# Attention over 8 batches: the expert correction applied to every tile's rows, or from the third batch on to the picked rows in DRAM

## What is computed

```
x = x + 0.5 * ffn(layernorm(x))
x = x + attn(layernorm(x))
x = x + 0.5 * ffn(layernorm(x))
```

```
merged = einsum('bked,bke->bed', tok, vals)
h = gelu([merged, 1] @ w1)
o = [h, 1] @ w2
out = zeros_like(x).at[b, flat_idx].add(o * vals)
```

## Time and profile before

| | |
|---|---|
| Median of 3 runs | 2297.79 us (2296.61 to 2299.26) |
| The profiled execution, its own time | 2299.73 us |
| Its span, first to last instruction | 2298.0 us |
| Gate | to about 170 us |
| Experts, first pass | about 170 to 930 us |
| Attention | about 930 to 1660 us |
| Experts, second pass, and the end | about 1660 to 2298 us |

### The profile page before, as it was taken

How to read it: one execution, slowest core, us unless ns; L and a number is a source line. 1 busy time by engine, 2 the same in 40 slices (tenths; PEclk the granted TensorE clock), 3 DMA queues, 4 the chain that set the end, 5 groups by cost and what they waited for, 6 DMA issues and landing times.

```text
span 2298.0 us, 44195 instructions
## 1 busy us (share of the span) xinstructions
PE 1981.2 (86%) x18664; PEld 1172.0 (51%) x18664; DVE 734.2 (32%) x1248; ACT 815.3 (35%) x1525; POOL 647.2 (28%) x783
## 2 busy tenths in 40 slices
PE   5789999999999999999999999999775666656666
PEld 3546666666666666676767767766521111111111
DVE  6731111111111111467677677677410000000011
ACT  6831121111111122477777777777510000000000
POOL 7620000000000000377777777777402000000002
PEclk9899999999999999999999999999987768887788
DMA  9999999999999999366554454444699999999997
GB/s 361 346 392 401 422 428 420 422 423 419 430 418 427 420 420 397 120 221 217 158 161 149 151 161 155 151 142 157 233 412 424 427 389 428 428 427 428 428 428 335
DMA packets 113844, 762.76 MB, mean 332 GB/s; under 512 B 21736, under 2 KB 21864, under 8 KB 76016
## 3 DMA queue, kind: packets, MB, share of 16 engines
q1 hardware_dynamic: 101552, 701.35, 76.9%
q10 hardware_dynamic: 9216, 50.34, 5.3%
q0 software_dynamic: 2880, 8.25, 0.9%
HBM read 648.65 MB, written 106.43 MB: 329 GB/s over the span
## 4 chain that ended last, share of the span: by engine, by line
PE 57%; DMA 23%; POOL 8%; ACT 5%; issue 4%; SPq 1%; DVE 1%; POOLq 0%; ACTq 0%; DVEq 0%
PE ps L316 53%; DMA big<-in_L_ffn_w 22%; PE ps L320 3%; POOL big L1475 2%; POOL s L1478 2%; DMA last_scratch<-idx 1%; SPq L18 1%; POOL big L1449 1%; ACT big L600 1%; POOL s L1460 1%; ACT big L1301 1%; POOL big L1480 1%; PE ps L787 1%; ACT big L585 1%; POOL big L1472 1%
## 5 line engine op out<-in xcount | busy, mean ns | idle before, releaser
L316 PE MATMUL ps<-big 128*32 128x512 f32 (+4 forms) x13792 | 985.2, 418 | 225.7 <-DMA big<-in_L_ffn_w 183.9
L316 PEld LDWEIGHTS ps<-big 128*32 128x32 f32 (+2 forms) x13792 | 385.9, 127 | 720.3 <-issue 383.4
L324 DVE TENSOR_TENSOR big<-ps,big 128x128 f32<-128x128 f32 (+3 forms) x375 | 343.7, 931 | 676.3 <-PE ps L787 509.6
L316 PE MATMUL ps<-wth,xth 128*128 128x512 f32 x768 | 311.8, 406 | 1.5 <-DVE xtl L324 1.5
L316 PE MATMUL ps<-wtl,xth 128*128 128x512 f32 x768 | 299.6, 390 | 0.0
L316 PE MATMUL ps<-wth,xtl 128*128 128x512 f32 x768 | 299.3, 390 | 0.0
L835 ACT COPY big<-ps 128x512 f32<-128x512 f32 x64 | 37.5, 586 | 650.8 <-PE ps L316 650.8
L1467 POOL TENSOR_SCALAR big<-big 128x1 f32<-128x1 f32 x64 | 12.3, 192 | 847.3 <-ACT ps L1279 844.8
L976 ACT ACTIVATE big<-ps,big 128x512 f32<-128x512 f32 x128 | 88.2, 689 | 371.8 <-PE ps L316 359.1
L985 DVE TENSOR_SCALAR big<-ps,big 128x512 f32<-128x512 f32 x64 | 48.0, 750 | 533.7 <-PE ps L316 533.7
L316 PE MATMUL ps<-wo,s 128*128 128x512 f32 x768 | 210.1, 409 | 3.4 <-ACT big L1349 1.9
(11 more groups left out here) (128 smaller groups left out, 1753.3 us busy)
## 6 DMA issues: line engine op xcount, KB each, us to landing
big<-in_L_ffn_w SPq DMA_DIRECT2D x254, 2048.0 KB, 18.0
p_scratch<-big ACTq DMA_DIRECT2D x64, 768.0 KB, 11.0
big<-p_scratch SPq DMA_DIRECT2D x64, 768.0 KB, 5.9
big<-in_L_attn_x SPq DMA_DIRECT2D x68, 256.0 KB, 3.0
xt_scratch<-big SPq DMA_DIRECT2D x16, 1024.0 KB, 8.2
big<-xt_scratch SPq DMA_DIRECT2D x16, 1024.0 KB, 15.8
x_weight_scratch<-big SPq DMA_DIRECT2D x64, 256.0 KB, 3.3
out_x<-big SPq DMA_DIRECT2D x64, 256.0 KB, 3.6
```

What stands on the lines that cost most here:

```text
L316: return nc.tensor.matmul(o, l, r, start=start, stop=stop, skip_group_check=True)
L324: return nc.vector.tensor_tensor(o, p, q, op)
```

## The change

The first two batches (TILED = 2) are corrected as before. For the others the correction is made on the picked rows alone, in DRAM, ahead of the tiles.

- `p_scratch` becomes, for each batch, a table of 1024 rows of 2080 floats: q, k, v (1536), the row's 32 expert weights, and its x (512). ACT's stores go to its first 1536 columns. SP copies x of the 48 later tiles from the input to the last 512 columns, DRAM to DRAM (`copy_x`), and stores the weights, kept in SBUF per batch (`MTK`), to the 32 columns between (`store_w`).
- In the first pass DVE finds the 8 picked positions per expert and batch (`rows_dve`, four operations at experts 2 and 3); SP writes them to DRAM, waits until they have landed, and reads them back in gather order (`rows_sp`, behind expert 6's chunk loads).
- For each batch b from 2 on, spread over the iterations before its tiles: POOL gathers its 256 picked rows of 8,320 bytes in two indirect DMAs at the end of iteration 8b-12 (place 4); PE transposes the gathered weights at place 6 and DVE copies them; PE corrects 128 rows each at places 7 and 0 (four matmuls each, as for a tile) and DVE adds them (two operations); POOL scatters 128 rows each at the end of places 1 and 2, the second scatter waiting until the first has landed. `load_p` and `load_x1` of the batch wait for both scatters.
- The four correction matmuls and the three DVE operations of tiles 16 to 63 go; DVE has one reduction of `X1` in their place, for the row sum. ACT no longer waits for the adds, and its square goes to SBUF. `load_m` of batches 2 to 7 goes.
- In the loop the rows' PE work stands, for n below 14, after the transposes of q; from n = 14 on it stands where the correction stood.
- The early loads of the second pass's chunks move: chunk 0 at n = 2, 4 at n = 16, 3 at n = 52, 1 and 2 at n = 54 and 58, 5 at n = 62 (before: 0, 1, 2 at n = 2, 6, 10 and 3, 4, 5 at n = 62).

```diff
@@ helpers
+        def turn(n, after):
+            b, k = divmod(n + 12 - after, 8)
+            return b if k == 0 and TILED <= b < B else None
...
@@ attention_sp
             def load_x1(n):
-                sp.dma_start(X1[n % 4], xs[n]).then_inc(d_x1[n % 4], 16)
+                if n >= 8 * TILED:
+                    sp.wait_ge(d_s, 32 * (n // 8 - TILED + 1))
+                sp.dma_start(X1[n % 4], xs[n] if n < 8 * TILED else x1d[n]).then_inc(d_x1[n % 4], 16)
...
@@ attention_pe
+            def rows_turn_pe(n):
+                if not (turn(n, 2) or turn(n, 3) or turn(n, 4)):
+                    return
+                pe.wait_ge(s_st, n + 1)
+                for s_ in (s_tk, s_tqv):
+                    pe.wait_ge(s_, min(n + 3, 8 * TILED))
+                pe.wait_ge(s_x1sq, min(n + 3, 8 * TILED))
+                if turn(n, 2):
+                    rows_weights_pe(pe, turn(n, 2))
+                for i in range(2):
+                    if turn(n, 3 + i):
+                        rows_pe(pe, turn(n, 3 + i), i)
...
-                if m < NT:
+                if m < 8 * TILED:
...
                     t.then_inc(s_c, 1)
+                else:
+                    rows_turn_pe(n)
...
+                if 0 <= n < 8 * TILED - 2:
+                    rows_turn_pe(n)
...
@@ attention_dve
+                elif m < NT:
+                    nc.vector.tensor_reduce(SX1[m % 2], X1[m % 4], AX.X, ALU.add).then_inc(s_x1, 1)
+                if turn(n, 2):
+                    rows_weights_dve(dve, turn(n, 2))
+                for i in range(2):
+                    if turn(n, 3 + i):
+                        rows_add_dve(dve, turn(n, 3 + i), i)
...
@@ attention_pool
+                if turn(n, 0):
+                    rows_gather_pool(pool, turn(n, 0))
+                for i in range(2):
+                    if turn(n, 5 + i):
+                        rows_scatter_pool(pool, turn(n, 5 + i), i)
...
+        def rows_sp(sp):
+            sp.wait_ge(s_pos, PO0 + 8)
+            for h in range(2):
+                sp.dma_start(idxd[h], IDX1[:, 8 * h:8 * h + 8]).then_inc(d_row, 16)
+            sp.wait_ge(d_row, RW0 + 32)
+            sp.dma_start(IDXG.rearrange("r (b i) -> r b i", i=2),
+                         idxd.rearrange("h p j -> (h p j)").rearrange("(b r i) -> r b i", r=128, i=2)).then_inc(d_idx, 16)
+
+        def rows_gather_pool(pool, b):
...
+            for i in range(2):
+                nc.gpsimd.indirect_dma_start(
+                    out=G[i], out_offset=None, in_=rowd[b],
+                    in_offset=bass.IndirectOffsetOnAxis(ap=IDXG[:, 2 * b + i:2 * b + i + 1], axis=0),
+                    bounds_check=S - 1, oob_is_err=False).then_inc(d_g, 16)
+
+        def rows_scatter_pool(pool, b, i):
+            pool.wait_ge(s_ga, GA0 + 2 * (b - TILED) + 2)
+            pool.wait_ge(d_s, 32 * (b - TILED) + 16 * i)
+            nc.gpsimd.indirect_dma_start(
...
+        def rows_weights_pe(pe, b):
+            pe.wait_ge(d_g, 32 * (b - TILED + 1))
+            for i in range(2):
+                for u in range(4):
+                    t = mm(ps[32 * u:32 * u + 32, 4, 128 * i:128 * i + 128], G[i][:, 3 * D:3 * D + E], IDN, True, True)
+            t.then_inc(s_gwT, 1)
...
+        def rows_pe(pe, b, i):
+            pe.wait_ge(s_gwt, GW0 + b - TILED + 1)
+            pe.wait_ge(d_os[b // 4], 16 * 16)
+            pe.wait_ge(s_ga, GA0 + 2 * (b - TILED) + i)
+            for u in range(4):
+                R_ = slice(32 * u, 32 * u + 32)
+                t = mm(ps[:, 4 + u, :], GWT[i][R_, :], OS[b][R_, :], True, True)
+            t.then_inc(s_gc, 1)
+
+        def rows_add_dve(dve, b, i):
+            dve.wait_ge(s_gc, GC0 + 2 * (b - TILED) + i + 1)
+            P3 = G[i][:, 0:3 * D].rearrange("p (u n) -> p u n", u=3)
+            X_ = G[i][:, 3 * D + E:XP]
+            tt(P3, ps[:, 4:7, :], P3, ALU.add)
+            nc.vector.scalar_tensor_tensor(out=X_, in0=ps[:, 7, :], scalar=0.5, in1=X_, op0=ALU.mult,
+                                           op1=ALU.add).then_inc(s_ga, 1)
```

147 lines of the change are left out of this document (119 added, 28 removed).

## The result

The changed kernel takes 2311.23 us (median of 5 runs, 2309.00 to 2315.63) where the kernel before takes 2297.79: the ratio is 1.006, with a 95% interval of 1.0048 to 1.0072. The change makes the kernel 0.6% slower. The profiled execution took 2309.56 us, of which 2306.9 are its span.

What follows compares the result with a forecast made beforehand. The attention's tile-to-tile path was taken as the bound, reaching the end one for one. Gains of 8.1 less losses of 8.1, 2.5 and 1 gave +3.5 on 2299.7, or 2303.2; the median lies 1.9 lower: 2301 us, range 2286 to 2327.

Steps and rivals of the forecast that it cites:

- the side that had the largest chance: Whole kernel: slower than the kernel before by over 0.2%, chance 0.45; faster had 0.25, same 0.30.
- The correction off the path: Attention: removing the tiles' correction gains 2.9 us per 8 tiles, and 3.9 us over the last ten tiles.
- The whole 1.07 comes off: Rival, attention: PE's full 1.07 us of correction per tile leaves the path, giving 2286 us; chance 0.25.
- The gathers at place 5: Two gathers delay POOL's L1438 and start q's transposes 0.7 us late; place 5 goes from +0.5 to -0.7.
- POOL pays by bytes: Rival, attention: gathers cost POOL 3.8 us each by bytes; 2360 us, 2330 at half the excess; chance 0.1.
- The scatters: Places 2 and 3: a scatter exceeds POOL's idle time by 0.74 us but is swallowed; cost 0 (0.4 at most).
- The landings: Place 6: PE waits 0.5 us per batch for gathered weights (0 to 3.8), 2.5 us in all.
- The landings decide: Rival: POOL waits at place 3 for the first scatter, PE at place 6 for gathers; 2327 us; chance 0.2.
- The first batches: Early attention: row work of batch 2 and batch 3's gather fall on tiles still corrected themselves; sum -8.1 us.
- about 1.2 comes back: First batches: about 1.2 us is regained, as PE no longer waits for POOL's L1478.
- The first pass: SP stops at expert 6 until two small DMAs land, delaying the next chunks: 1 us, between 0 and 12.
- The second pass: Its stream starts when attention frees buffers, so attention's gain or loss reaches the end one for one.

Runs made afterwards that it cites:

- no rows at all: The changed kernel without gathers, weights, products, adds and scatters of the picked rows: 2280.50 us, ratio 0.9920 to the kernel before.
- the second execution: The changed kernel run again unchanged, on the chip of the follow-up runs: 2314.86 us, ratio 1.0059 to the kernel before.
- the ten with the transfer in one part: Ten executions of kernels whose SP issues the whole index transfer at expert 6: first pass 807.9 to 812.3 us.
- the transfer in two parts: Changed kernel with indirect DMAs inside POOL's iteration, scatters one iteration earlier, and the index transfer's second part at expert 9: 2296.22 us, ratio 0.9983.
- the run with the first scatter moved: The changed kernel with only the first scatter moved into POOL's iteration at place 1, the second left at place 2's end: 2307.85 us, ratio 1.0044.
- both kinds of DMA in the gap: The changed kernel with gathers and scatters issued one per iteration between L1561 and L1564, where POOL waits for ACT: 2299.19 us, ratio 0.9998.
- the run with a pair of gathers more: The changed kernel with the third batch's two gathers issued in iteration 3 and again in iteration 4: 2318.51 us, ratio 1.0074.

## Why the prediction was right, and where it was wrong

The forecast was 2301 us, nearly level; the time is 2311.23. It lies in the range (2286 to 2327) and on the side that had the largest chance, 0.45. That is partly luck: 0.30 of this chance stood on two rivals, late landings and a POOL that pays by bytes, and neither happened. Half of the sum's terms were right; one that was put at 0 makes up the whole miss. Step by step:

- **The correction off the path: right.** 3.9 us for the last ten tiles, measured 3.9; 2.9 for eight tiles, measured 3.0 with no rows at all (87.09 to 84.06), and right place by place. "The whole 1.07 comes off" is out.
- **The gathers at place 5: right.** Forecast -0.7, measured -0.8 and, in the second execution, -1.1. The working of the 0.7 has a slip: 1193.34 + 1.03 - 0.20 + 1.05 gives 1195.2 and not 1195.4, so its rows stand for some 0.5, and part of the closeness is chance. POOL's indirect DMAs took 1.00 to 1.12 us each (the first of the program 1.31), at 8,320 bytes a row as at 2,176: "POOL pays by bytes" is out.
- **The scatters: this step failed.** The forecast was "At place 2 DVE is later still: 0. At place 3 L1449 takes 1.85 us where it takes 1.05 elsewhere, stretched by DVE's work beside it, so a later start shortens it: 0 (0.4 at most)". The two scatters cost 1.16 us at place 3 and 0.39 at place 4 (12.24 to 11.08 and 10.58 to 10.19 when they are left out), 1.5 us in each of six batches, 9 in all. The reading looked at one engine's next operation only. It did not follow POOL's order one iteration on, to ACT and the low part of k, and took a stretched operation for slack. L1449 did get its 1.05 us back, as forecast, but a shorter operation ahead of it was stretched in its place. The Trainium skill ("SBUF — State Buffer", Who interferes with whom) was cited for the scatter being swallowed. The rule itself shows here, as L1527 stands until DVE's L435 ends (1.18 us instead of 0.19). But by it the delay would be swallowed only if no operation of POOL stood between the scatter and the end of L435; two short ones do, and the delays add.
- **The landings.** 2.5 us were put down for PE's wait at place 6; there was none. "The landings decide" did not happen either, though it was near: with the second scatter issued sooner it had to wait until 7.2 to 11.2 us after the first, and the changed kernel leaves 11.4 to 11.7 (the prediction had 10.1). From its issue a gather took 7.7 to 12.5 us. The Trainium skill's estimate ("DMA: Bandwidth & Descriptors", Anatomy of one DMA), 6.9 us for both, gave the right answer, no wait, with too short a time: from the first issue to the second landing there are 11.1 to 14.1 us.
- **The first batches: 8.1 forecast, 11.2 measured.** The three iterations with rows were right in their sum: 7.9 forecast, 7.9 measured (2.7, 2.3 and 2.9, where 1.9, 3.0 and 3.0 were put down), with waits of 1.16 and 0.53 at n = 7. In the second execution n = 6 was 0.5 shorter. What failed is that "about 1.2 comes back", which nothing shows, and the third batch's scatters (n = 11 and 12, +1.3) and gathers (n = 4 and 5, +1.3 where 0.7 was put down).
- **The first pass: right in kind, 1 forecast.** 1.2 in the profiled execution, 1.0 to 5.5 over the ten with the transfer in one part. It is the wait for a chunk that the prediction named, 0.85 us at 328.85 in one trace and 3.38 in the other; with the transfer in two parts it is gone.
- **The second pass: right.** Whatever the attention lost reached the end one for one; from mask 63 on the two traces differ by 0.1 us.

So the profiled 8.9 us are 11.2 + 3.9 + 1.2 - 3.9 - 3.4 (scatter of the gate) - 0.1. Taking out the gate's luck gives 12.3. The medians differ by 13.4; the 1.1 between the two is within what the first pass scatters. Against the forecast's +3.5 that is 8.8 too much. The scatters alone are 9.0. The other misses nearly cancel: 1.2 that didn't come back, 0.6 at the third batch's gathers and 1.2 at place 7 (five times 0.24, for which no cause was looked for), against 2.5 for landings that cost nothing. Two of the five runs took 2315 us. Whether they had lower-clock stretches in the attention isn't known, as they have no trace; their mean clocks, 0.939 and 0.935, lie at and just under the 0.939 of the fastest run.

## What to carry to other kernels

An operation added to an engine that is half idle costs by its place in that engine's order: the same 24 DMAs cost 13 to 15 us of attention more at the ends of POOL's iterations than in the gap where POOL waits for ACT. Before putting such an operation at 0, follow what it delays through every engine for one full iteration, and check for each wait that you add how much time is left ahead of it, not only whether it is hidden. An exact reading of what is removed (2.9 us forecast, 3.0 measured) is worth little when the other side of the sum is read one step deep.

## What the runs showed of the hardware

- **POOL's issue of an indirect DMA** of 128 rows takes 1.00 to 1.12 us at 2,176 and at 8,320 bytes a row (1.31 for the first of the program), with 0.30 to the next.
- **It can stand.** In two kernels without scatters POOL stood 7.39 and 8.62 us before one and the same gather, and the second pass's 8th and 16th gathers stand over 20 us in the kernel before as in the changed one. Wherever the trace has the landings, POOL goes on 0.56 to 0.58 us after one of the gathers before has landed, nearly always the last one. Without scatters it is the 8th, 15th, 22nd and 28th indirect DMA of the program. With scatters among them none stood in the attention except where the program itself waits for a landing, and a wait on the gathers' semaphore did not help; the rule behind the count is open.
- **A short operation of POOL beside a DVE operation with two inputs in SBUF** is held until that ends: 0.19 us became 1.18 (L1527), and in the run with the first scatter moved, where L1531 was the one that met L435, its 0.55 became 1.62. It goes the other way too: L435 took 2.11 us instead of 1.28 where a long operation of POOL had begun just before it (n = 19 with both kinds of DMA in the gap). Such a stretched row is no slack: moving it later hands the hold to the operation in front of it.
- **PE's clock sometimes fell behind short waits.** After 1.65 and 0.18 us of waiting, 1.1 us of matmuls between them, the granted clock was 0.61 over the next 4 us, so part of them ran at 1.2 and part at 2.4 GHz, and the iteration was 1.6 us longer. The same waits at n = 19 and 27 of that execution had no such effect, and in the run without scatters a wait of 1.63 us at place 3 had none in any batch. So the waits alone do not decide it, and that they are the cause is not shown. It happened three times in that execution and twice in the run with a pair of gathers more, around a wait of 2.48 us and behind waits of 0.81 and 0.47. In the traces of the kernel before, the changed one (both) and the version with both kinds of DMA in the gap the granted clock is 1.00 all the way from the first mask to the last.
